# The low part of the softmax maxima on GpSimd, the high part by a one-tensor maximum on VectorE

## The reference

```python
x = x + layernorm(attention(layernorm(x)))   # 16 heads of 8, 4 KV heads, causal, W_qkv, W_out, biases
x = x + layernorm(layernorm(x) @ (ternary(W) * alpha).T + bias)
# attention: softmax(q k^T / sqrt(8)) v, over the keys up to the row's own
# layernorm: (x - mean) / sqrt(var + 1e-5), no weights
```

## Time and profile before

| what | value |
|---|---|
| median of three runs | 456.02 us |
| the profiled execution, its own time | 456.64 us |
| its span, first to last instruction | 454.8 us |
| TensorE matmul busy | 398.6 us (88%) |
| VectorE busy | 394.7 us (87%) |
| ScalarE busy | 333.3 us (73%) |
| GpSimd busy | 296.3 us (65%) |
| mean granted TensorE clock | 0.97 |

### The profile page before, as it was taken

The page is one execution under the profiler, slowest core; times in us unless marked ns, Lnnn a source line. Parts: engine busy times, 40 slices in busy tenths (PEclk is TensorE's granted clock), DMA queues, the critical chain, the costliest instruction groups (busy, mean ns, idle before and its releaser), DMA issues.

```text
span 454.8 us, 19223 instructions
## 1 busy us (share of the span) xinstructions
PE 398.6 (88%) x7430; PEld 280.8 (62%) x7430; DVE 394.7 (87%) x1180; ACT 333.3 (73%) x609; POOL 296.3 (65%) x552
## 2 busy tenths in 40 slices
PE   0569999999999999999999999999999999998551
PEld 0336766676666676666666666676676777764330
DVE  5957878999999999999999999999999989995442
ACT  0333877777888888888888888888888888888332
POOL 2622323657677877777777777787777666766676
PEclk9999999999999999999999999999999999999855
DMA  7176465524434344444344444443444543421342
GB/s 190 35 121 94 103 107 133 127 75 85 77 72 80 81 76 81 78 76 79 66 70 77 76 72 80 81 75 80 82 74 85 114 84 69 87 77 30 111 145 73
DMA packets 72307, 39.59 MB, mean 87 GB/s; under 512 B 13048, under 2 KB 68056, under 8 KB 72216
## 3 DMA queue, kind: packets, MB, share of 16 engines
q1 hardware_dynamic: 70880, 37.70, 41.7%
q10 hardware_dynamic: 1336, 0.66, 0.5%
HBM read 13.67 MB, written 4.72 MB: 40 GB/s over the span
## 4 chain that ended last, share of the span: by engine, by line
PE 47%; DVE 29%; issue 9%; DMA 4%; POOL 3%; SPq 3%; ACT 2%; POOLq 0%; DVEq 0%; ACTq 0%
DVE M L619 13%; PE ps_mx L843 13%; PE ps_y L816 11%; PE ps_w L872 7%; PE ps_st L792 7%; PE ps_w L913 5%; DVE stats L584 4%; DVE xn L602 3%; DMA QS<-part 3%; DVE A L666 2%; DVE mv L594 2%; PE ps_w L893 2%; DVE Mp L683 2%; DVE F L674 2%; SPq L260 2%
## 5 line engine op out<-in xcount | busy, mean ns | idle before, releaser
L619 DVE TENSOR_REDUCE M<-ps_mx 128x2 f32<-128x512 f32 (+3 forms) x352 | 210.5, 626 | 14.2 <-PE ps_mx L843 13.5
L419 ACT ACTIVATE PT<-ps_st 128x1024 f32<-128x1024 f32 (+1 forms) x192 | 165.3, 884 | 20.4 <-PE ps_st L792 20.3
L843 PE MATMUL ps_mx<-KS,QS 112*64 112x128 bf16 (+2 forms) x2560 | 132.7, 228 | 15.9 <-DVE M L619 11.6
L843 PEld LDWEIGHTS ps_mx<-KS,QS 112*64 112x64 bf16 x2560 | 89.6, 112 | 60.9 <-DVE M L619 37.2
L358 POOL TENSOR_TENSOR rstd<-vareps,mhalf 128x2 f32<-128x2 f32 x128 | 93.0, 727 | 10.0
L792 PE MATMUL ps_st<-QS,KS 114*64 114x256 bf16 (+1 forms) x1024 | 97.9, 300 | 0.2 <-DMA QS<-MpT 0.2
L816 PE MATMUL ps_y<-PT,VB 128*32 128x256 f32 (+3 forms) x2048 | 90.4, 304 | 1.3 <-ACT PT L419 1.0
L356 POOL TENSOR_TENSOR vareps<-mv,eps 128x2 f32<-128x2 f32 x128 | 25.9, 203 | 73.3 <-DVE mv L594 73.3
L816 PEld LDWEIGHTS ps_y<-PT,VB 128*32 128x32 f32 x2048 | 46.7, 109 | 28.6 <-issue 9.4
L393 POOL TENSOR_TENSOR rest<-QK,part 128x512 f32<-128x512 f32 x32 | 38.2, 1193 | 24.3 <-ACT part L448 24.1
L792 PEld LDWEIGHTS ps_st<-QS,KS 114*64 114x64 bf16 x1024 | 52.0, 111 | 1.5 <-DMA QS<-MpT 0.5
(11 more groups left out here) (63 smaller groups left out, 512.9 us busy)
## 6 DMA issues: line engine op xcount, KB each, us to landing
QS<-part SPq DMA_DIRECT2D x192, 64.0 KB
rden<-rec_dram SPq DMA_DIRECT2D x32, 256.0 KB
X<-in_x SPq DMA_DIRECT2D x7, 512.0 KB, 6.3
out<-X SPq DMA_DIRECT2D x7, 512.0 KB, 5.4
KS<-part SPq DMA_DIRECT2D x32, 96.0 KB
KS<-part SPq DMA_DIRECT2D x32, 64.0 KB
KS<-part SPq DMA_DIRECT2D x32, 32.0 KB
QS<-MpT SPq DMA_DIRECT2D x32, 16.0 KB
```

What stands on the lines that cost most here:

```text
L419: nc.scalar.activation(PT[(b * CHUNKS + n) % TILES][:, 0:512 * banks], ps_st[n % 2][:, 0:banks, :].rearrange("p a c -> p (a c)"), ACT.Exp, ...
L619: nc.vector.tensor_reduce(M[b % 2][:].rearrange("p k g i -> p (k g) i")[:, 2 * kv:2 * kv + pairs, i], ps_mx[(b * BANKS + n) % 2][:, 0:pair ...
L843: last = pe.matmul(ps_mx[(b * BANKS + n) % 2][64 * one:64 * one + 64, at:at + w], q[:, h, BL * i:BL * i + BL], k[:, kv, blocks, :], start= ...
```

## The change

VectorE's split_max, two two-input instructions, becomes high_max, one reduction over an inner axis of length 1 that writes the bfloat16 high part. The low part, the subtraction, is the new low_max on GpSimd, at the head of its step t for batch t-6, ahead of the addition of A. It waits for the high part. The order of everything else, the count of s_mp and the buffers stay.

```diff
@@ GpSimd
+            def low_max(b):
+                if on(b):
+
+                    gp.wait_ge(s_mp, 2 * b + 1)
+                    gp.tensor_tensor(Mp[:, 1, :], M[b % 2][:].rearrange("p k g i -> p (k g i)"), Mp[:, 0, :],
+                                     ALU.subtract).then_inc(s_mp, 1)
...
             def step(t):
+                low_max(t - 6)
                 add_normed(t - 10, A2, s_a2, s_x1)
                 third(t - 4)
                 inverse(t, 0)
@@ VectorE
-            def split_max(b):
-                if on(b):
-                    m = M[b % 2][:].rearrange("p k g i -> p (k g i)")
+            def high_max(b):
+                if on(b):
 
                     dve.wait_ge(s_mx, BANKS * b + BANKS)
                     free(dve, b, s_mt_ps)
-                    nc.vector.tensor_tensor(Mp[:, 0, :], m, m, ALU.max).then_inc(s_mp, 1)
-                    dve.wait_ge(s_mp, 2 * b + 1)
-                    nc.vector.tensor_tensor(Mp[:, 1, :], m, Mp[:, 0, :], ALU.subtract).then_inc(s_mp, 1)
+                    nc.vector.tensor_reduce(Mp[:, 0, :], M[b % 2][:].rearrange("p k g i -> p (k g i)").unsqueeze(2), AX_X,
+                                            ALU.max).then_inc(s_mp, 1)
...
                 maxima(t - 7, 10)
-                split_max(t - 7)
+                high_max(t - 7)
                 moments(t - 1, 0)
```

## The result

The changed kernel took 458.63 us in the median of 19 runs (456.55 to 460.96), the kernel before 456.31 in 19 runs beside it (455.0 to 458.09). The ratio is 1.0049, 95% interval 1.0032 to 1.0066: slower, by about 2.3 us. I had forecast 442.3, range 439.5 to 453.5. The profiled execution took 456.55 us, span 454.8, the same span as in the profile before.

A forecast was written before the change was run, and what follows sets the result against it. A GpSimd–VectorE ring through yn bound the kernel at 12.35 us per batch; TensorE's 11.74 would replace it. -12.80 +0.7 -0.55 -1.1 = -13.75: 456.64 to 442.9, or 442.3 at the runs' median level; range 439.5 to 453.5.

The forecast's parts named there:

- TensorE's floor of 11.74: Time TensorE alone needs for a full step, read late in the run: 11.74 us, forecast as the new period.
- VectorE's new work of 10.96: VectorE's work per period after the change, forecast to fall from 12.18 to about 10.96 us, below TensorE's 11.74.
- The price of the reduction, 0.19, and of low_max, a push of 0.22: Per batch, VectorE's new reduction takes 0.19 us; low_max pushes GpSimd's queue by 0.22 us.
- The ring through yn: Steady loop from A over GpSimd's queue to yn, then the next A: 7.32 + 1.27 + 3.76 = 12.35 us, the old period.
- No new wait ahead of low_max: On GpSimd, the high part is ready at +4.44 us after A's start, before GpSimd reaches low_max at +4.58.
- norm_x at +7.43: VectorE's norm_x, ready at +7.11, is held by TensorE's x1 until 7.43 us after the start of A.
- yn at +7.54: GpSimd's yn moves from 7.32 to 7.54 us after the start of A, 0.11 behind norm_x.
- the rival: yn goes first or between the two norm_x instructions; norm_x ends behind it; period 12.57 us, total 459.7, chance 0.14.
- rstd held to norm_x's end as at 237.96: GpSimd's rstd, just ahead of yn, held from +7.57 to norm_x's end at +8.03 us; yn ends about +9.3.
- The startup row: At startup GpSimd's rest took 2.32 us, ending behind the second of two back-to-back VectorE copies; cited for VectorE keeping the port.
- The last batch, -1.1: In the last batch the old L685 (1.21 us) and some 0.2 of L683 leave the chain: -1.1 us.
- The two shorter steps before it, -0.55: Two shorter steps before the last wait for maxima on the chain; estimated gain 0.55 us.

The follow-up runs named there:

- the kernel with three buffers: The changed kernel with three buffers instead of two for xn1, so norm_x need not wait for x1 of two batches before: 444.46 us, ratio 0.9716.

## Why the prediction was wrong, step by step

- *TensorE's floor of 11.74, VectorE's new work of 10.96.* Right: 11.74 and 10.92 in the kernel with three buffers.
- *The price of the reduction, 0.19, and of low_max, a push of 0.22.* Right: 0.19, and 0.20 (0.25 long). One reason that I gave was not a like case, though: the maxima read PSUM (ps_mx in their rows), the new reduction reads SBUF.
- *The ring through yn.* Right: a push of yn by 0.15 made the period of the kernel before longer by 0.15. The loop over the Mp instructions lay only 0.10 below it.
- *No new wait ahead of low_max.* Right in the steady part; over the run GpSimd waited for the high part 9 times, 12.6 us in total, almost all of it in the filling and draining.
- *norm_x at +7.43 because x1 holds it, yn at +7.54.* Right to 0.02 us.
- **The step that failed:** "So the order of norm_x and yn is reversed, by 0.11 us, and norm_x takes 0.60." norm_x did start first, by 0.09, but it took 1.70 and ended behind yn. Starting first was not enough. The lead has to be about 0.34: at 0.09 neither instruction of norm_x passed, at 0.23 one did, at 0.33 to 0.35 it went either way, at 0.55 both did. With that lead, had by a third buffer or by an idle memset, the forecast came true within 2.2 us (444.46 and 444.2 for 442.3). I had put the deciding point of the rival near +7.5; it lies near +7.2.
- *rstd held to norm_x's end as at 237.96, which would have widened the margin.* Wrong: in the changed kernel rstd took 0.70, with norm_x begun 0.57 behind its start. With three buffers, norm_x begun 0.31 behind it, it still took 0.70, and it was yn that paid, with 1.38. In the row at 237.96 norm_x began only 0.19 behind rstd.
- *The startup row as evidence that VectorE keeps the port over two instructions in a row*. It misled. The second norm_x instruction follows the first without a gap, and yn still came between them. On this the Trainium skill, SBUF — State Buffer, "Who interferes with whom", was nearer: it gives the shared pair to whoever issues first for the whole instruction, and by the runs too the race is run for each instruction by itself. But the starts in the profile do not say who was first: at 231.41 against 231.50 the later start won. Why GpSimd waited for both copies at the startup stays open.
- *The rival.* Its mechanism, place and period (12.57 forecast, 12.56 measured) came out, and its total nearly (459.7; 458.63 measured, as the end gave more than 1.1 back). I gave it 0.14, with a margin of 0.11 us against a race whose edge no row before had measured.
- *The last batch, -1.1.* Right: -1.06. *The two shorter steps before it, -0.55:* too large; they became 0.18 shorter (10.82 and 10.29 before, 10.69 and 10.24 after).

The caution of the Trainium skill, Perfetto Trace Analysis, "Optimizing Scalar/DVE Operations", that moving work between these two engines may not help, agrees with the result. It is not the moved work, though, that contends: low_max took its 0.25 undisturbed, and a run without it gained no more than 0.3%.

## What to carry to other kernels

When two engines contend for a port, an instruction that waits takes the length of the other's, and a microsecond saved ahead of it turns into waiting: ask where the next contended instruction lands, not how busy the engine is. A start that is 0.1 us earlier in the profile was no lead here, and of several instructions in a row each has to win for itself; give the last of them a margin, by freeing what holds it (a buffer) or by delaying the other side, and try the order before counting on it. A queue that is three quarters busy can set the period when the end of one of its instructions releases the other engine.

## What the runs showed of the hardware that I had not expected

- VectorE's TENSOR_SCALAR of 128x128 float32, SBUF to SBUF, waited for a GpSimd TENSOR_TENSOR that started up to 0.10 us behind it and never for one that started 0.15 behind it or later; the second of a pair had its edge at 0.08, so that the pair needed a lead of about 0.34 us to pass whole.
- When GpSimd ran two halves in a row, one waiting VectorE instruction came through behind each: norm_x's two ended 0.08 behind the first half and 0.08 behind the second.
- A GpSimd MEMSET held it up too: the pair took 0.84 instead of 0.60 when begun 0.68 us into a MEMSET of 1.38.
- The reduction with an inner axis of 1 wrote 32 bfloat16 from 32 float32 in 0.185 to 0.189 us in all 32 batches; the two-input form took 0.19 to 0.43 beside GpSimd.
